# Selective scan of a fused four-layer block: TensorE makes the scan's input for both halves from dt*u turned beforehand

## The chip, the cores and the metric

The kernel runs on one core of a Trainium2 chip. The metric is the device time in microseconds (us) of the one launch that does everything. Engines are named as in the profile: PE is TensorE (its weight loads are PEld), DVE is VectorE, ACT is ScalarE, POOL is GpSimd, SP is SyncE, which issues DMAs. L1942 is line 1942 of the kernel before.

## The reference

The input is 4 sequences of 1024 tokens of 128 channels. Four layers follow one another, each on a layer norm of the running sum: attention, a mixture of 8 experts, a Mamba layer, a second mixture of experts. Only the Mamba layer matters here, cut to its core:

```python
xz = (x @ fc1_w.T + fc1_b) @ in_proj_w.T
xc, z = jnp.split(xz, 2, axis=-1)          # 256 inner channels each
u = silu(causal_conv4(xc, conv_w) + conv_b)
x_dbl = u @ x_proj_w.T                     # 8 columns for dt, 16 for B, 16 for C
dt = softplus(low8 @ dt_proj_w.T + dt_proj_b)
...                                        # for each of 16 states n, each channel c, along time t:
h[t] = exp(dt[t] * A[c, n]) * h[t - 1] + dt[t] * u[t] * B[t, n]
y[t] += h[t] * C[t, n]                     # summed over the 16 states
out = ((y + u * D) * silu(z)) @ out_proj_w.T @ fc2_w.T + fc2_b
```

## The kernel before, in words

Everything is float32 unless said otherwise. Each engine has its own instruction stream, written by hand, and semaphores order them; a block ends with a barrier of all engines. The Mamba layer is four blocks, one after another.

`mamba_in` (the input stage) works on 8 chunks of 512 tokens. The 256 inner channels are two halves of 128 partitions. Its first loop makes `u` and `silu(z)`. Its second loop makes, for each chunk: the low-rank product (`low_rank`, L1719: B, C and the 8 rows for dt, in one PSUM bank), `dt` (`project_dt`, L1726, then softplus as Abs, Exp and Ln on ACT at L1625 to L1630, `join` on DVE at L1674 and an addition on POOL at L1574), B turned so that tokens lie on partitions (`turn_b`, written inside `project_dt` at L1730, kept as `m.bt`), the rows of B and C written to DRAM (L1551), and B and C split into three bfloat16 parts whose sum is the float32 value (L1618, L1667, L1570, L1678, L1680; kept as `m.bc`).

`mamba_scan` (the scan stage) runs over 4 sequences x 16 states = 64 states, in pairs, and for each state over the two halves. A tile of one half and one state is 128 channels x 1024 tokens. For each of the 128 such tiles DVE runs one `tensor_tensor_scan` (L1942) along time. It needs two things: the decay, which ACT makes as exp(dt*A) (L1903), and the input dt*u*B. The two halves get their input in different ways:

- half 0: PE spreads the row of B over the partitions (`spread`, L1800: two bfloat16 matmuls of 96 rows and 512 columns), and DVE multiplies it in PSUM by dt*u (`scan_input`, L1932).
- half 1: PE makes the whole input (`make_x`, L1829): for each of 8 blocks of 128 tokens one float32 matmul with dt*u turned (tokens on partitions) as the stationary operand and a diagonal matrix of B as the moving one. ACT makes these diagonals (`diagonals`, L1883). The dt*u of the next sequence is made on POOL (L1982) and turned on PE one block at a time (L1812), stored by ACT (L1897).

After a scan POOL multiplies the state by the row of C (`weigh`, L1979), and PE adds the product into the running sum in PSUM (`add`, L1839, two float32 matmuls of 512 columns with the identity, for each tile). `skip` (L1846) adds u*D, twice in each sequence; `gate` on DVE (L1947) ends a sequence. The order of PE's stream in a pair is written out: add, spread, add, make_x, add, spread, add, make_x. The input banks in PSUM are single for each half: `spread` and `make_x` of the next state wait until the scan of this one has read them (`scanned`). `weigh` has one tile for each half, so it waits for `add` of the state before (`summed`).

The chunk order of the input stage's second loop is that of `ahead`: `low_rank` and `split` of chunk c+1 stand in front of `project_dt` and `join` of chunk c.

Of the kernel before, what the change touches and what calls it, by code (L numbers as in the profile page):

```python
# [15 lines left out]
P = 128  # L16
# [1453 lines left out]
def mamba_loads(nc, ctx, early, g):  # L1470
# [4 lines left out]
    m.sel_b = m.tensor("sel_b", [6 * NS, NS, P], g.w["sel_b"], BF16)  # L1475
# [3 lines left out]
    m.bc = sb("bc", [6 * NS, N], BF16)  # L1479
# [16 lines left out]
def mamba_in(nc, g, m):  # L1496

    with ExitStack() as ctx:
# [10 lines left out]
        rest = sb("rest", [2 * NS, 2, CH])  # L1509
        part1 = sb("part1", [2 * NS, 2, CH], BF16)  # L1510
# [7 lines left out]
        low_done, part0_ready, low_ready, rest_ready, part1_ready, part2_ready, dt_done, top_ready, soft_steps, dt_ready, a_steps = map(sem, (  # L1518
            "low_done", "part0_ready", "low_ready", "rest_ready", "part1_ready", "part2_ready", "dt_done", "top_ready",
            "soft_steps", "dt_ready", "a_steps"))  # L1520
        block = ctx.enter_context(nc.Block())
        CONV = KC * DI
        X_BANK, Z_BANK, LOW_BANK, DT_BANK, TURN_BANK = 0, 4, 0, 2, 6
# [19 lines left out]
        @block.sync  # L1543
        def _(sp):
            for k in range(2):
                sp.sem_inc(c_written[k], 16)
            with sp.Fori(0, B) as b:
                for k in range(CPB):
                    c = CPB * b + k
                    sp.wait_ge(whole_ready, c + 1)  # L1550
                    sp.dma_start(g.bc_rows[:, tokens(c)], bc_whole[:, k, :]).then_inc(c_written[k], 16)  # L1551
            for k in range(2):
                sp.wait_ge(c_written[k], 16 + 16 * B)

        @block.gpsimd
        def _(pool):
            pool.memset(xc[:, 0, :, 0:KC - 1], 0.0).then_inc(pad_set, 1)
            pool.wait_ge(m.loaded, m.all)

            pool.tensor_tensor(g.X[:, :, :], g.X[:, :, :], fc2_b[:, :].rearrange("p (a e) -> p a e", a=1).to_broadcast([P, NT, E]),  # L1560
                               ALU.add).then_inc(pool_seen, 1)

            with pool.Fori(0, B) as b:
                for k in range(CPB):
                    c = CPB * b + k

                    pool.wait_ge(part2_ready, c + 1)
                    pool.wait_ge(rest_ready, 2 + c + 1)
                    pool.sem_inc(pool_seen, 1)
                    pool.tensor_copy(part1[:, k, :], rest[:, k, :]).then_inc(part1_ready, 1)  # L1570
                    pool.wait_ge(top_ready, 2 + c + 1)
                    pool.wait_ge(soft_steps, 3 * (c + 1))
                    pool.sem_inc(pool_seen, 1)
                    pool.tensor_tensor(m.dt[:, :, tokens(c)], top[:, k, :, :], soft[:, k, :, :], ALU.add).then_inc(dt_ready, 1)  # L1574

        @block.scalar
        def _(act):
# [35 lines left out]
            def part0(b, k, c):  # L1613
                act.wait_ge(low_done, c + 1)
                act.wait_ge(c_written[k], 16 * b + 16)
                act.wait_ge(b_turned, c + 1)
                act.activation(bc_whole[:, k, :], PS[0:2 * NS, LOW_BANK + k, :], ACT.Copy).then_inc(whole_ready, 1)
                act.activation(m.bc[0:2 * NS, tokens(c)], PS[0:2 * NS, LOW_BANK + k, :], ACT.Copy).then_inc(part0_ready, 1)  # L1618

            def softplus(b, k, c):  # L1620

                act.wait_ge(dt_done, 2 + c + 1)
                act.wait_ge(dt_ready, c + 1)
# [7 lines left out]
            ahead(act, part0, softplus)  # L1631
            act.wait_ge(b_turned, 2 + NCH)
            act.activation(m.bt[:, :], PS[:, TURN_BANK, :], ACT.Copy).then_inc(a_steps, 1)
            act.wait_ge(a_steps, 3)

        @block.vector
        def _(dve):
            dve.sem_inc(conv_steps, 2 * CONV)
            dve.sem_inc(dt_ready, 2)
            dve.sem_inc(part2_ready, 2)  # L1640
# [19 lines left out]
            def split(b, k, c):  # L1660
                dve.wait_ge(low_done, c + 1)
                dve.wait_ge(dt_done, c - 1 + 2)
                dve.tensor_copy(low[2 * NS:, k, :], PS[2 * NS:2 * NS + R, LOW_BANK + k, :]).then_inc(low_ready, 1)
                dve.wait_ge(part0_ready, c + 1)
                dve.wait_ge(part1_ready, c + 1)
                dve.wait_ge(part2_ready, c + 1)
                dve.tensor_tensor(rest[:, k, :], PS[0:2 * NS, LOW_BANK + k, :], m.bc[0:2 * NS, tokens(c)], ALU.subtract).then_inc(rest_ready, 1)  # L1667

            def join(b, k, c):
                dve.wait_ge(dt_done, 2 + c + 1)  # L1670
                dve.wait_ge(dt_ready, c + 1)
# [5 lines left out]
                dve.wait_ge(rest_ready, 2 + c + 1)  # L1677
                dve.tensor_copy(m.bc[2 * NS:4 * NS, tokens(c)], rest[:, k, :])  # L1678
                dve.wait_ge(part1_ready, 2 + c + 1)
                dve.tensor_tensor(m.bc[4 * NS:6 * NS, tokens(c)], rest[:, k, :], part1[:, k, :], ALU.subtract).then_inc(part2_ready, 1)  # L1680
            ahead(dve, split, join)
            dve.wait_ge(a_steps, 2)
            dve.wait_ge(dt_ready, 2 + NCH)
            dve.wait_ge(part2_ready, 2 + NCH)

        @block.tensor
        def _(pe):
            pe.sem_inc(u_ready, 2 * DI)
            pe.sem_inc(dt_done, 2)
            pe.sem_inc(part1_ready, 2)  # L1690
            pe.sem_inc(z_ready, 2)
            pe.sem_inc(rest_ready, 2)
            pe.sem_inc(top_ready, 2)
            pe.sem_inc(b_turned, 2)
# [21 lines left out]
            def low_rank(b, k, c):  # L1716
                pe.wait_ge(rest_ready, c + 1)
                for half in range(DI):
                    last = pe.matmul(PS[0:2 * NS + R, LOW_BANK + k, :], x_proj[:, half, :], m.u[:, half, tokens(c)], start=half == 0, stop=half == DI - 1)  # L1719
                last.then_inc(low_done, 1)  # L1720

            def project_dt(b, k, c):
                pe.wait_ge(low_ready, c + 1)
                pe.wait_ge(top_ready, c + 1)
                for half in range(DI):
                    last = pe.matmul(PS[:, DT_BANK + 2 * k + half, :], dt_proj[2 * NS:, half, :], low[2 * NS:, k, :], start=True, stop=True)  # L1726
                last.then_inc(dt_done, 1)
                pe.wait_ge(whole_ready, c + 1)
                for i in range(TPC):
                    last = pe.matmul(PS[:, TURN_BANK, bass.ds(c * (TPC * NS) + i * NS, NS)], bc_whole[0:NS, k, i * P:(i + 1) * P], g.ident[0:NS, 0:NS],  # L1730
                                     start=True, stop=True)
                last.then_inc(b_turned, 1)
            ahead(pe, low_rank, project_dt)


def mamba_scan(nc, g, m):


    with ExitStack() as ctx:
# [3 lines left out]
        h = g.xnT[:, :].rearrange("p (k d t) -> p k d t", k=2, d=DI)  # L1743
        dtu, decay = sb("dtu", [P, DI, T]), sb("decay", [P, 2, DI, T])
        c_rows, ch = sb("c_rows", [P, C_RING, T]), sb("ch", [P, DI, T])
        diag = sb("diag", [P, DI, P])
        dtu_turns, b_diag = sb("dtu_turns", [P, 2, TB, P]), sb("b_diag", [P, 2, TB, P])
        b_spread, decay_ready, dtu_ready, other_dtu_ready, input_ready, scanned, ch_ready, summed, gated, diag_ready = map(sem, (
            "b_spread", "decay_ready", "dtu_ready", "other_dtu_ready", "input_ready", "scanned", "ch_ready", "summed", "gated", "diag_ready"))
# [602 lines left out]
```

## Time and profile before

| what | us |
|---|---|
| median of 3 runs (lowest, highest) | 1429.58 (1429.04, 1433.34) |
| the profiled execution, its own time | 1432.1 |
| its span, from the first to the last instruction | 1430.3 |
| second loop of the input stage: first low-rank matmul | at 813.10 |
| scan stage: first instruction | at 856.90 |
| scan stage: last gate begins | at 1256.57 |

The profiled execution lies 2.5 above the median, and its own time 1.8 above its span. Everything below is read on the axis of the span. PE is busy for 89% of the span, DVE for 78%, ACT for 58% and POOL for 41%. The mean clock granted to TensorE is 0.933 of full speed. A busy PE in the profile includes the modelled ends of matmuls, which overlap; the distance from start to start is what a group of matmuls takes.

### The profile page before, as it was taken

The page shows a single profiled execution, that of the slowest core. Times are in us where ns is not written, and L with a number is a line of the kernel's source. Part 1 is how long each engine was busy: PE and PEld are TensorE (multiplying, and loading weights), DVE is VectorE, ACT ScalarE, POOL GpSimd, SP SyncE. Part 2 cuts the span into 40 slices and gives each one's busy share as a digit, 9 for nine tenths or more (in the row PEclk, how much of TensorE's full clock was granted, in tenths as well). Part 3 has the DMA queues.
Part 4 walks back from the last instruction along what each step waited for, and adds up shares of the span by engine and source line. Part 5 has one row for each costly group of instructions (what it writes and reads, how often), then busy time and mean ns, then how long its engine had stood idle before and what let it go on. Part 6 is the DMA issues. An engine that isn't in the chain of part 4 may idle for free. (4 is left out here: it accounts for less than half of the span.)

```text
span 1430.3 us, 23953 instructions
## 1 busy us (share of the span) xinstructions
PE 1268.5 (89%) x8534; PEld 662.8 (46%) x8534; DVE 1111.4 (78%) x1328; ACT 830.7 (58%) x1596; POOL 590.2 (41%) x442
## 2 busy tenths in 40 slices
PE   4937899999899889899978779999999999966998
PEld 2412333333334445354444235655656655555565
DVE  4769899999898547756555888989999999954554
ACT  2524899899798632132224788777778778502221
POOL 2320000010102166556744067788798788720000
PEclk9966999999999989999997878999999999985999
DMA  4331111311211173234420003222222222110221
GB/s 108 113 109 35 54 54 52 109 60 50 76 44 42 41 175 105 88 108 117 115 60 15 4 13 102 89 89 87 87 78 89 89 89 89 59 29 11 67 60 42
DMA packets 70751, 103.76 MB, mean 73 GB/s; under 512 B 12734, under 2 KB 42246, under 8 KB 70646
## 3 DMA queue, kind: packets, MB, share of 16 engines
q1 hardware_dynamic: 69350, 101.05, 23.4%
q10 hardware_dynamic: 1296, 1.33, 0.4%
q8 instruction: 64, 1.05, 0.3%
q14 instruction: 41, 0.34, 0.1%
HBM read 88.32 MB, written 13.63 MB: 71 GB/s over the span
## 5 line engine op out<-in xcount | busy, mean ns | idle before, releaser
L638 DVE TENSOR_REDUCE att_found<-PS 128x2 f32<-128x1024 f32 (+2 forms) x288 | 333.2, 1219 | 18.9 <-PE PS L747 17.1
L714 ACT ACTIVATE att_prob<-PS 128x512 f32<-128x512 f32 x576 | 313.5, 596 | 46.2 <-PE PS L769 34.4
L1979 POOL TENSOR_TENSOR ms_ch<-xnT,ms_c_rows 128x1024 f32<-128x1024 f32 x128 | 300.3, 2366 | 81.9 <-PE PS L1839 68.5
L1942 DVE TENSOR_TENSOR_SCAN xnT<-ms_decay,PS 128x1024 f32<-128x1024 f32 x128 | 287.0, 2276 | 17.6 <-PE PS L1829 8.7
L1839 PE MATMUL PS<-ms_ch,ident_sb 128*128 128x512 f32 x512 | 241.5, 594 | 1.2 <-POOL ms_ch L1979 1.2
L788 PE MATMUL PS<-att_prob,att_v 128*32 128x256 f32 (+1 forms) x2560 | 184.9, 376 | 2.8 <-ACT fr_out L703 2.6
L1903 ACT ACTIVATE ms_decay<-m_dt,m_a 128x1024 f32<-128x1024 f32 x128 | 145.8, 1144 | 54.8 <-DVE xnT L1942 53.3
L1883 ACT ACTIVATE ms_b_diag<-ident_sb,m_bt 128x128 f32<-128x128 f32 x512 | 155.7, 387 | 0.0
L747 PE MATMUL PS<-kr,qr 55*128 55x128 bf16 (+4 forms) x1152 | 121.4, 292 | 30.9 <-PEq L260 15.7
L1829 PEld LDWEIGHTS PS<-ms_b_diag,ms_dtu_turns 128*128 128x128 f32 x1024 | 122.6, 194 | 32.0 <-issue 29.7
L1829 PE MATMUL PS<-ms_b_diag,ms_dtu_turns 128*128 128x128 f32 x1024 | 127.7, 279 | 6.6 <-issue 5.4
L769 PE MATMUL PS<-qr,kr 55*128 55x128 bf16 (+4 forms) x1152 | 115.5, 279 | 15.2 <-ACT att_prob L714 8.3
L1839 PEld LDWEIGHTS PS<-ms_ch,ident_sb 128*128 128x128 f32 x512 | 91.7, 190 | 75.1 <-issue 61.7
L1262 ACT ACTIVATE f_h<-PS,e_w_b 128x512 f32<-128x512 f32 x64 | 44.0, 687 | 138.2 <-PE PS L1413 135.0
L747 PEld LDWEIGHTS PS<-kr,qr 48*128 48x128 bf16 (+1 forms) x1152 | 39.7, 97 | 138.2 <-issue 88.8
L1243 POOL TENSOR_TENSOR f_yT<-f_yT,f_prod 128x512 f32<-128x512 f32 x56 | 71.0, 1268 | 70.8 <-DVE f_prod L1355 69.4
L1345 DVE SCALAR_TENSOR_TENSOR f_x3s<-PS,e_w_b,f_mask_row 128x512 f32<-128x512 f32 x64 | 48.0, 750 | 61.5 <-PE PS L1417 60.8
L1231 POOL TENSOR_TENSOR f_xm<-xnT,f_gate_row 128x512 f32<-128x512 f32 x64 | 81.2, 1270 | 13.3 <-DMA f_gate_row<-gate_rows_dram 9.8
L788 PEld LDWEIGHTS PS<-att_prob,att_v 128*32 128x32 f32 x2560 | 55.2, 109 | 63.1 <-issue 53.9
L1932 DVE TENSOR_TENSOR PS<-ms_dtu,PS 128x1024 f32<-128x1024 f32 x64 | 77.4, 1210 | 4.5 <-PE PS L1800 2.4
L1422 PE MATMUL PS<-f_h,e_w_w 128*128 128x512 f32 x128 | 66.3, 599 | 8.5 <-DVE f_prod L1355 8.4
L1413 PE MATMUL PS<-f_xm,e_w_w 128*128 128x512 f32 x128 | 67.8, 612 | 4.1 <-POOL f_xm L1231 4.1
(232 smaller groups left out, 1634.6 us busy)
## 6 DMA issues: line engine op xcount, KB each, us to landing
ms_c_rows<-bc_rows_dram SPq DMA_DIRECT2D x64, 512.0 KB, 3.6
f_gate_row<-gate_rows_dram SPq DMA_DIRECT2D x64, 256.0 KB, 3.4
f_mask_row<-mask_rows_dram SPq DMA_DIRECT2D x64, 128.0 KB, 3.1
qk_parts_dram<-qkv_parts SPq DMA_DIRECT2D x48, 128.0 KB, 1.9
heads_dram<-fr_out SPq DMA_DIRECT2D x16, 256.0 KB, 2.6
f_mask_row<-mask_rows_dram SPq DMA_DIRECT2D x64, 64.0 KB, 3.2
qr<-qk_parts_dram SPq DMA_DIRECT2D x32, 96.0 KB
qr<-qk_parts_dram SPq DMA_DIRECT2D x96, 32.0 KB
```

Source lines behind the costliest of these rows:

```text
L638: dve.tensor_reduce(found[:, :, pair, first:first + (n - 1) * step + 1:step], PS[:, bank:bank + 2, :].rearrange("p r (w n) -> p r w n", w= ...
L714: act.activation(prob[:, step % PROB_RING * GH + h, :], PS[:, SCORE_BANK + unit % SCORE_RING, :], ACT.Exp, scale=float(D) ** -0.5).then_in ...
L747: last = pe.matmul(PS[:, MAX_BANK + 2 * (m % 2) + r, at:at + n], rows(qr, count, i, pair, r, q_block * P, P), rows(kr, count, i, pair, r, ...
L769: last[r] = pe.matmul(PS[:, SCORE_BANK + (unit + r) % SCORE_RING, col:col + w], rows(kr, count, i, pair, r, j * P, P), rows(qr, count, i, ...
L788: last = pe.matmul(PS[VW * h:VW * (h + 1), VALUE_BANK, q - half * CH:q - half * CH + w], v1[:, i % 2, half, h, j, :], prob[:, step % PROB_ ...
L1231: pool.tensor_tensor(xm[:, e % XM_RING, :], xnT[:, c * CH:(c + 1) * CH], gate_row[:, e % ROW_RING, :], ALU.mult).then_inc(xm_ready, 1)
L1829: last = pe.matmul(PS[:, X_BANK + 2 + k // TPC, k % TPC * P:(k % TPC + 1) * P], dtu_turns[:, b % 2, k, :], b_diag[:, odd, k, :], start=Tru ...
L1839: last = pe.matmul(PS[:, Y_BANK + 2 * half + q, :], g.ident[:, :], ch[:, half, q * CH:(q + 1) * CH], start=j == 0 and not odd, stop=j == J ...
L1883: last = act.activation(b_diag[:, odd, i, :], g.ident[:, :], ACT.Identity, scale=m.bt[:, at:at + 1])
L1903: act.activation(decay[:, odd, half, :], m.dt[:, half, sequence(p // JB)], ACT.Exp, scale=m.a[:, half, n:n + 1]).then_inc(decay_ready, 1)
L1942: dve.tensor_tensor_scan(h[:, odd, half, :], decay[:, odd, half, :], inputs(half), 0.0, ALU.mult, ALU.add).then_inc(scanned, 1)
L1979: pool.tensor_tensor(ch[:, half, :], h[:, odd, half, :], c_rows[:, s % C_RING, :], ALU.mult).then_inc(ch_ready, 1)
```

## The change

In the input stage, the split of B and C into bfloat16 parts is gone, with its loads (`sel_b`, `m.bc`). Instead DVE multiplies dt by u (`times_u`, both halves of a chunk in one instruction), PE turns the product (`turn_dtu`, 8 transposes a chunk), and ACT stores the turned half 0 and DVE the turned half 1 (`store_turns`), for all four sequences. The low-rank product has one PSUM bank in place of two, and only the rows of C go to DRAM. In the scan stage PE makes the input of both halves by `make_x`; `spread`, `scan_input` and the turns inside the scan are gone. The scan writes the state over its decay, in a ring of three. A half is added 1.5 states (half 1: two) after the newest input in PE's stream. The ring of C rows has 4 places for 3. The diff, cut to its core:

```diff
 def mamba_in(nc, g, m):
...
+            def store_turns(c):
+                act.wait_ge(dtu_turned, DI * c + 1)
+                act.activation(m.dtu_turns[:, c * TPC:(c + 1) * TPC, 0, :], PS[:, DTU_BANKS[0], :].rearrange("p (i c) -> p i c", c=P),
+                               ACT.Copy).then_inc(dtu_stored[0], 1)
+
+            store_low(0)
+            for c in range(NCH):
+                if c + 1 < NCH:
+                    store_low(c + 1)
+                softplus(c)
+                if c >= 2:
+                    store_turns(c - 2)
...
+            def times_u(c):
+                dve.wait_ge(dt_ready, c + 1)
+                if c >= 2:
+                    dve.wait_ge(dtu_turned, DI * (c - 1))
+                dve.tensor_tensor(dtu[:, c % 2, :, :], m.dt[:, :, tokens(c)], m.u[:, :, tokens(c)], ALU.mult).then_inc(dtu_ready, 1)
...
+            split(0)
+            for c in range(NCH):
+                if c + 1 < NCH:
+                    split(c + 1)
+                join(c)
+                if c >= 1:
+                    times_u(c - 1)
+                if c >= 2:
+                    store_turns(c - 2)
...
+            def turn_dtu(c):
+                pe.wait_ge(dtu_ready, c + 1)
+                for half in range(DI):
+                    if c >= 1:
+                        pe.wait_ge(dtu_stored[half], c)
+                    for i in range(TPC):
+                        last = pe.transpose(PS[:, DTU_BANKS[half], i * P:(i + 1) * P], dtu[:, c % 2, half, i * P:(i + 1) * P], g.ident[:, :])
+                    last.then_inc(dtu_turned, 1)
...
 def mamba_scan(nc, g, m):
...
+            def make_x(s, half):
+
+                pe.wait_ge(b_diag_ready, through(s, 1))
+                if s > 0:
+                    pe.wait_ge(scanned, through(s - 1, half))
+                for k in range(TB):
+                    last = pe.matmul(PS[:, X_BANK + 2 * half + k // TPC, k % TPC * P:(k % TPC + 1) * P], m.dtu_turns[:, s // NS * TB + k, half, :],
+                                     b_diag[:, s % 2, k, :], start=True, stop=True)
+                last.then_inc(x_made, 1)
...
             pe.wait_ge(diag_ready, DI)
-            spread(0, 0)
-            first_turns()
             make_x(0, 0)
...
+            make_x(0, 1)
+            for s in range(STATES):
+                if s + 1 < STATES:
+                    make_x(s + 1, 0)
+                if s >= 2:
+                    add(s - 2, 1)
+                if s + 1 < STATES:
+                    make_x(s + 1, 1)
+                if s >= 1:
+                    add(s - 1, 0)
+            add(STATES - 2, 1)
+            add(STATES - 1, 0)
+            add(STATES - 1, 1)
...
+            for part in range(CPB):
+                diagonals(0, part)
+            for s in range(STATES):
+                for half in range(DI):
+                    decays(s, half)
+                    if s + 1 < STATES:
+                        diagonals(s + 1, half)
...
+            def scan(s, half):
+                dve.wait_ge(decay_ready, through(s, half))
+                dve.wait_ge(x_made, through(s, half))
+                dve.tensor_tensor_scan(decay_then_h(s, half), decay_then_h(s, half), inputs(half), 0.0, ALU.mult, ALU.add).then_inc(scanned, 1)
...
+            for s in range(STATES):
+                b, n = divmod(s, NS)
+                for half in range(DI):
+                    scan(s, half)
+                    if n == 1 and b > 0:
+                        gate(b - 1, half)
...
+            for s in range(STATES):
+                pool.wait_ge(c_in[s % C_RING], C_BASE + 16 * (s // C_RING + 1))
+                for half in range(DI):
+                    pool.wait_ge(scanned, through(s, half))
+                    if s >= 1:
+                        pool.wait_ge(summed, through(s - 1, half))
+                    pool.tensor_tensor(ch[:, half, :], decay_then_h(s, half), c_rows[:, s % C_RING, :], ALU.mult).then_inc(ch_ready, 1)
```

PE's stream in the middle of the scan stage before, over two states (a row is one instruction of the program with its line, what it writes and reads, and its shape; x8 means eight in a row):

```order
L1829 MATMUL PS<-ms_b_diag,ms_dtu_turns 128x128 x8
L1839 MATMUL PS<-ms_ch,ident_sb 128x512 x2
L1800 MATMUL PS<-m_bc,m_w_sel_b 128x512 x2
L1839 MATMUL PS<-ms_ch,ident_sb 128x512 x2
L1829 MATMUL PS<-ms_b_diag,ms_dtu_turns 128x128 x8
L1839 MATMUL PS<-ms_ch,ident_sb 128x512 x2
L1800 MATMUL PS<-m_bc,m_w_sel_b 128x512 x2
L1839 MATMUL PS<-ms_ch,ident_sb 128x512 x2
```

The same place after the change, over two states again (line 1825 is `make_x`, 1835 is `add`):

```order
L1825 MATMUL PS<-ms_b_diag,m_dtu_turns 128x128 x8
L1835 MATMUL PS<-ms_ch,ident_sb 128x512 x2
L1825 MATMUL PS<-ms_b_diag,m_dtu_turns 128x128 x8
L1835 MATMUL PS<-ms_ch,ident_sb 128x512 x2
L1825 MATMUL PS<-ms_b_diag,m_dtu_turns 128x128 x8
L1835 MATMUL PS<-ms_ch,ident_sb 128x512 x2
L1825 MATMUL PS<-ms_b_diag,m_dtu_turns 128x128 x8
L1835 MATMUL PS<-ms_ch,ident_sb 128x512 x2
```

In each state the two bfloat16 matmuls of `spread` have given their place to a second group of eight float32 matmuls of `make_x`; the two groups of `add` are still there.

DVE's stream at a like place before:

```order
L1932 TENSOR_TENSOR PS<-ms_dtu,PS 128x1024
L1942 SCALAR_TENSOR_TENSOR xnT<-ms_decay,PS 128x1024 x2
L1932 TENSOR_TENSOR PS<-ms_dtu,PS 128x1024
L1942 SCALAR_TENSOR_TENSOR xnT<-ms_decay,PS 128x1024 x2
L1932 TENSOR_TENSOR PS<-ms_dtu,PS 128x1024
```

And after (line 1889 is the scan, over three states of the ring, with line 1894, the gate, where a sequence ends):

```order
L1889 SCALAR_TENSOR_TENSOR xnT<-xnT,PS 128x1024 x4
L1889 SCALAR_TENSOR_TENSOR ms_one_state<-ms_one_state,PS 128x1024
L1894 TENSOR_TENSOR m_u<-PS,m_sz 128x1024
L1889 SCALAR_TENSOR_TENSOR ms_one_state<-ms_one_state,PS 128x1024
L1894 TENSOR_TENSOR m_u<-PS,m_sz 128x1024
```

The multiplication in front of every second scan is gone from DVE; two scans a state are left.

PE's stream in the input stage's second loop after the change, over two chunks (1732 is `low_rank`, 1742 `project_dt`, 1748 `turn_b`, 1758 `turn_dtu`):

```order
L1732 MATMUL PS<-m_u,m_w_x_proj 40x512 x2
L1742 MATMUL PS<-mi_low,m_dt_proj 128x512 x2
L1748 MATMUL PS<-ident_sb,mi_bc_whole 128x16 x4
L1758 MATMUL PS<-ident_sb,mi_dtu 128x128 x8
L1732 MATMUL PS<-m_u,m_w_x_proj 40x512 x2
L1742 MATMUL PS<-mi_low,m_dt_proj 128x512 x2
L1748 MATMUL PS<-ident_sb,mi_bc_whole 128x16 x4
L1758 MATMUL PS<-ident_sb,mi_dtu 128x128 x8
```

The first three rows of a chunk were there before (L1719, L1726, L1730); the eight transposes are new.

## Rows read from the trace of the kernel before

**Rows 1.** Groups by line, 861 to 1252 us: busy us, mean ns, idle before.

```profile
L1979 POOL TENSOR_TENSOR ms_ch<-xnT,ms_c_rows 128x1024 f32<-128x1024 f32 x127 | 298.0, 2366 | 81.9 <-PE PS L1839 68.5 <-DVE xnT L1942 13.1
L1942 DVE TENSOR_TENSOR_SCAN xnT<-ms_decay,PS 128x1024 f32<-128x1024 f32 x128 | 287.0, 2276 | 17.6 <-PE PS L1829 8.7 <-ACT ms_decay L1903 0.6
L1839 PE MATMUL PS<-ms_ch,ident_sb 128*128 128x512 f32 x504 | 237.5, 593 | 0.0
...
L1903 ACT ACTIVATE ms_decay<-m_dt,m_a 128x1024 f32<-128x1024 f32 x128 | 145.8, 1144 | 54.8 <-DVE xnT L1942 53.3
L1829 PE MATMUL PS<-ms_b_diag,ms_dtu_turns 128*128 128x128 f32 x1024 | 127.7, 279 | 6.6 <-issue 5.4 <-ACT ms_dtu_turns L1889 1.2
...
L1932 DVE TENSOR_TENSOR PS<-ms_dtu,PS 128x1024 f32<-128x1024 f32 x64 | 77.4, 1210 | 4.5 <-PE PS L1800 2.4 <-POOL ms_dtu L1982 2.0
...
L1846 PE MATMUL PS<-m_u,ms_diag 128*128 128x512 f32 x32 | 15.0, 592 | 0.0
```

**Rows 2.** Timeline of PE in the scan stage: start us, length us, line, count.

```profile
1020.52 1.95 PE L1829 MATMUL PS<-ms_b_diag,ms_dtu_turns 128*128 128x128 f32 x16
1022.31 1.88 PE L1839 MATMUL PS<-ms_ch,ident_sb 128*128 128x512 f32 x4
1024.03 0.60 PE L1800 MATMUL PS<-m_bc,m_w_sel_b 96*128 96x512 bf16 x2
1024.46 1.88 PE L1839 MATMUL PS<-ms_ch,ident_sb 128*128 128x512 f32 x4
1026.18 0.27 PE L1812 MATMUL PS<-ident_sb,ms_dtu 128*128 128x128 f32 x1
1026.29 1.95 PE L1829 MATMUL PS<-ms_b_diag,ms_dtu_turns 128*128 128x128 f32 x16
```

**Rows 3.** Windows: length, busy of PE, PEld, DVE, ACT, POOL, then granted clock.

```profile
751.00:757.00 6.00, 4.44 (x16) 2.86 (x16) 5.15 (x20) 1.93 (x4) 6.00 (x7) 0.50 0.36 82
...
827.00:832.00 5.00, 5.00 (x20) 1.75 (x19) 4.57 (x8) 4.91 (x8) 2.91 (x2) 1.00 0.05 13
...
842.00:847.00 5.00, 4.97 (x17) 2.74 (x18) 4.57 (x8) 4.71 (x8) 3.29 (x3) 0.50 0.10 26
...
900.00:1240.00 340.00, 333.63 (x1493) 199.25 (x1492) 320.12 (x174) 258.83 (x579) 271.53 (x117) 1.00 0.25 87
```

**Rows 4.** Timeline of the input stage's second loop, PE and DVE.

```profile
820.32 1.91 PE L1719 MATMUL PS<-m_u,m_w_x_proj 128*40 x4
...
824.07 1.91 PE L1719 MATMUL PS<-m_u,m_w_x_proj 128*40 x4
```

**Rows 5.** Timeline of the same loop, all engines.

```profile
834.53 1.41 DVE L1674 TENSOR_SCALAR mi_xc<-PS,m_w_dt_b 128x512 f32<-128x512 f32 x2 [0.29 <-ACT mi_conv L1625]
...
838.80 1.41 DVE L1674 TENSOR_SCALAR mi_xc<-PS,m_w_dt_b 128x512 f32<-128x512 f32 x2 [0.29 <-ACT mi_conv L1625]
...
850.20 1.26 ACT L1625 ACTIVATE mi_conv<-PS,m_w_dt_b 128x512 f32<-128x512 f32 x2 [0.37 <-PE PS L1726]
...
853.90 2.45 POOL L1574 TENSOR_TENSOR m_dt<-mi_xc,mi_conv 128x1024 f32 x1 [1.15 <-ACT mi_conv L1630]
```

**Rows 6.** Groups by line, 812 to 856.9 us.

```profile
L1628 ACT ACTIVATE mi_conv<-mi_conv 128x1024 f32<-128x1024 f32 x8 | 8.5, 1057 | 0.3
...
L1663 DVE COPY mi_low<-PS 8x512 f32<-8x512 f32 x8 | 5.5, 683 | 2.2 <-PE PS L1719 2.0
...
L1617 ACT ACTIVATE mi_bc_whole<-PS 32x512 f32<-32x512 f32 x8 | 4.6, 574 | 3.0 <-PE PS L1719 3.0
```

**Rows 7.** Timeline of the first microseconds of the scan stage.

```profile
856.95 2.81 DVE L1927 TENSOR_TENSOR ms_dtu<-m_dt,m_u 128x1024 f32<-128x1024 f32 x2 [2.79 <-PEq L1498]
858.21 2.45 ACT L1883 ACTIVATE ms_b_diag<-ident_sb,m_bt 128x128 f32<-128x128 f32 x8
...
862.70 3.78 PE L1829 MATMUL PS<-ms_b_diag,ms_dtu_turns 128*128 128x128 f32 x16 [1.23 <-ACT ms_dtu_turns L1889]
```

**Rows 8.** Timeline of the last gate of the scan stage.

```profile
1256.57 1.23 DVE L1947 TENSOR_TENSOR m_u<-PS,m_sz 128x1024 f32<-128x1024 f32 x1 [1.08 <-PE PS L1839]
```

More of the change, by code:

```diff
@@ L1561, in _ @@
                                ALU.add).then_inc(pool_seen, 1)
[L1563 to L1574, printed above, removed]
+            for c in range(NCH):
+                pool.wait_ge(top_ready, c + 1)
+                pool.wait_ge(soft_steps, 3 * (c + 1))
+                pool.tensor_tensor(m.dt[:, :, tokens(c)], top[:, c % 2, :, :], soft[:, c % 2, :, :], ALU.add).then_inc(dt_ready, 1)
         @block.scalar
@@ L1833, in add @@
-            def add(p, odd, half):
-                b, j = divmod(p, JB)
-                if j == 0 and not odd and b > 0:
-                    pe.wait_ge(gated, DI * (b - 1) + half + 1)
-                pe.wait_ge(ch_ready, scans(p, odd, half))
-                for q in range(CPB):
-                    last = pe.matmul(PS[:, Y_BANK + 2 * half + q, :], g.ident[:, :], ch[:, half, q * CH:(q + 1) * CH],
-                                     start=j == 0 and not odd, stop=j == JB - 1 and bool(odd))
+            def make_x(s, half):
[6 more added lines that the diff above has]
+                last.then_inc(x_made, 1)
@@ L1841, in add @@
+            def add(s, half):
+                b, n = divmod(s, NS)
+                if n == 0 and b > 0:
+                    pe.wait_ge(gated, through(b - 1, half))
+                pe.wait_ge(ch_ready, through(s, half))
+                for q in range(CPB):
+                    last = pe.matmul(PS[:, Y_BANK + 2 * half + q, :], g.ident[:, :], ch[:, half, q * CH:(q + 1) * CH], start=n == 0, stop=n == NS - 1)
                 last.then_inc(summed, 1)
[L1843 to L1846 removed]
+                if n == NS // 2 + half:
+                    for q in range(CPB):
+                        pe.matmul(PS[:, Y_BANK + 2 * half + q, :], diag[:, half, :], m.u[:, half, b * T + q * CH:b * T + (q + 1) * CH], start=False, stop=False)
@@ L1874, in _, with diagonals @@
             act.preload_act_table(ACT.Exp)
-            def diagonals(p, odd):
-                n, b = 2 * p % NS + odd, p // JB
-                if p > 0:
-                    act.wait_ge(x_made, states(p - 1, odd))
-                for i in range(TB):
+            def diagonals(s, part):
+                b, n = divmod(s, NS)
+                if s >= 2:
+                    act.wait_ge(x_made, through(s - 2, 1))
+                for i in range(part * TPC, (part + 1) * TPC):
                     at = NS * (TB * b + i) + n
-                    last = act.activation(b_diag[:, odd, i, :], g.ident[:, :], ACT.Identity, scale=m.bt[:, at:at + 1])
+                    last = act.activation(b_diag[:, s % 2, i, :], g.ident[:, :], ACT.Identity, scale=m.bt[:, at:at + 1])
```

310 lines of the change are left out of this document (87 added, 223 removed).

## The prediction, made before the changed kernel ran

> **What bounds the kernel now.** I read the page first. It ranks DVE's scan and PE's additions near the top and gives no stage. So I asked for the groups by line inside the scan stage, then for PE's timeline there, then for the windows with the granted clock, then for the timelines of the loop before it.
>
> The scan stage runs from 856.9 [rows 7] to the end of the last gate, 1256.57 + 1.23 = 1257.8 [rows 8]: 400.9 us. Over 64 states DVE spends 287.0 on scans and 77.4 on the multiplication for half 0 [rows 1], 5.76 a state (2 x 2.276 + 1.21). It looks like the bound: its idle time before scans is 17.6 in all. But PE is as full. From start to start in [rows 2], `make_x` takes 1022.31 - 1020.52 = 1.79, an `add` 1024.03 - 1022.31 = 1.72, `spread` 0.43, the other `add` 1.72, a transpose 0.11; then the next state's `make_x` starts. These five follow one another with no gap, and their sum is 5.77, from 1020.52 to 1026.29. So here PE and DVE are level at about 5.77 a state, and I read the busy share of PE (333.6 of 340 [rows 3]) as real and not as a product of modelled ends. POOL needs 2 x 2.37 = 4.73 a state and waits for `add` (68.5 in all), ACT 2 x 1.14 + 2.45 = 4.74 (two decays [rows 1], eight diagonals [rows 7]) and waits for the scans (53.3). Both have over one microsecond to spare.
>
> **The change, part by part.**
>
> *Scan stage, DVE.* 64 multiplications of 1.21 go: 77.4 less, 4.55 a state left. That is worth something only if nobody else needs 5.77.
>
> *Scan stage, PE.* A state loses `spread` (0.43) and, in 24 of the 64 states, a transpose of 0.11; it gains a second `make_x` of the same shape, operands and kind, 1.79. New cycle: 2 x 1.79 + 2 x 1.72 = 7.02, against 5.77. Times 64 that is 449.3. The `skip` matmuls stay: 32 records are 8 groups of 4, each as long as an `add`, so 13.8. PE's whole work is 463.1. Before it was 64 x 5.66 + 13.8 + 24 x 0.11 + about 2 for the first turns = 381, in a stage of 401; DVE's was 287.0 + 77.4 + 8 gates of 1.23 + 2.8 = 377. The 20 above these sums was lost because two full engines wait for one another through single input banks.
>
> Can PE run its 7.02 without gaps? Call t the end of `make_x`(s+1, half 0). Then PE has `add` (s-2, half 1) until t+1.72, `make_x`(s+1, half 1) until t+3.51, `add`(s-1, half 0) until t+5.23, and `make_x`(s+2, half 0), which wants scan(s+1, half 0): t to t+2.3, nearly 3 early. `make_x`(s+2, half 1) starts at t+8.7 and wants the other scan, over at t+5.8. `weigh`(s, half 0) can start at t+5.3 (its tile is free after the `add`), ends by t+7.7, and its `add` comes at t+10.5. The decays go into a tile whose `weigh` ended more than 9 before. So no wait is left in the steady state, DVE idles 2.5 a state, and what was lost to coupling should mostly not recur. Where a sequence ends, two gates stand between scans: DVE waits for the last `add` of half 0 (t+5.3), then for that of half 1 (t+8.8), so the next scans are late: about 0.3 of PE, three times, 1 in all.
>
> The in-place scan and the third ring place have no row. Bounds: nothing, and 1.22 more a scan (7.02 shared by two, less 2.28) before DVE would be the bound. I take nothing, since even half as much again would hide under PE.
>
> *Start and end.* The first `make_x` needs ACT's table load and eight diagonals: 1.28 + 2.45 [rows 7], so it starts about 3.9 after the stage's start. PE has been idle and its clock is low: the first `make_x` of before took 3.78 from 862.70 [rows 7] where it takes 1.79 later. I count the first two at that length, 4.0 more than in the sum. Filling costs 0.6 (the second state's `make_x` waits for the first scans), the end 3.5 (`weigh`, 2.37, is no longer covered between the last additions; from the last `make_x` the chain add, weigh, add, weigh, add is 13 to 14 long and the bare additions 10.3), and the last gate 1.4. Stage: 3.9 + 463.1 + 4.0 + 1 + 0.6 + 3.5 + 1.4 = 477.5, against 400.9: **+76.6**.
>
> *Input stage.* Before, PE alone could turn a chunk in 824.07 - 820.32 = 3.75 [rows 4], and the loop ran at 838.80 - 834.53 = 4.27 [rows 5], set by DVE and ACT. Now PE has 8 transposes more, 0.11 each: 4.63. ACT: 0.57 for the low rows, 1.26 + 1.06 + 1.06 of softplus [rows 5, 6], 0.57 for the turned half (the same 512 columns; half 0 of a chunk), with gaps 4.6. DVE: 0.68 + 1.41 + 1.40 (2.81 for two of 128x1024 [rows 7]) + 0.68 = 4.2. Three engines within 0.4 of one another, and one bank for the low rows where there were two: I take 4.8 a chunk, between 4.65 (PE without a wait) and 5.3. Over the 7 steps from the first to the last softplus, with the first `project_dt` a microsecond later than before because the second low-rank product waits for the bank, the last softplus begins at 854.7 for 850.20 [rows 5]. After it: 3.4 of softplus, 2.45 on POOL [rows 5] as before, and new behind it `times_u` 1.4, 8 transposes (1.9 at the low clock), a store 0.7. Before, the stage ended with POOL's addition. So 4.5 + 4.0 is 8.5, less 0.5 of gaps that overlap: **+8**, with bounds of 4 and 13.
>
> What goes from the input stage (two ACT and DVE copies, POOL's cast, the 384 KB load of `sel_b`) is counted in these cycles; the loads themselves ended under the normalisation and delayed nothing.
>
> **Sum.** 76.6 + 8 is 84.6. I shave 1 for the clock rising sooner in the first two `make_x` than I counted: +83.5. The profiled execution's own 1432.1 becomes 1515.6; on the median 1429.58 it is **1513**.
>
> A rule weighed against this. The loop of the normalisation does only transposes on PE, and its granted clock is 0.50 [rows 3], the lower of the two levels (1.2 GHz), though PE is busy 4.44 of 6.00 there. In the input stage before, the clock was full from 817 and fell to 0.50 once PE had begun to wait for DVE in each chunk [rows 3]. The Trainium skill, "TensorE: Matmul & The Clock Gate", Part 4 (PE-mode transpose), says that transposes do not count as PE-busy for the clock in the way that matmuls do. The row of the normalisation agrees. By that rule the eight transposes a chunk would be a pause to the clock in every chunk; it makes the second rival below likelier.
>
> **The rivals.**
>
> *The clock falls in the input stage* (0.2). Before, it fell after four chunks with the PE at 3.75 of 4.27. If the new loop loses it too, a chunk costs PE 2 x 4.63 = 9.3 for 4.8, and four chunks cost 18 more: 1531. For it: the low window at 842 and the transposes. Against: PE is now nearly the slowest engine of this loop and hardly waits. With two such chunks it is 1522.
>
> *The scan stage couples after all* (0.1). The addition of half 1 now comes late, and `weigh` waits for it. If POOL were late by 0.2 a state (rows: it runs 4.73 of 7.02, so this needs handovers of more than a microsecond each), the stage is 13 longer: 1526.
>
> *Faster: PE was not full* (0.03). If the starts in [rows 2] only show PE pushed by DVE's pace and the second `make_x` fitted into slack, DVE's 4.55 would rule: 64 x 1.21 = 77 less, 8 more of input stage, 1360. It decides at the point where two `make_x` and two additions together take less than 5.77; for that `make_x` would have to cost 1.17. Against: a stretch of float32 matmuls with no gap between groups, at full clock, has no slack to give.
>
> *No net change* (0.02): `make_x` at 1.17 to 1.2, or DVE losing more to coupling before than I see. The same evidence speaks against it.
>
> The rest, 0.65, is the forecast, 1513, whose own bounds are 1504 (input stage +4, no loss at the boundaries and at the end) and 1521 (input stage +13, 0.05 more a state).
>
> **How the numbers follow.** Likeliest 1513. The range reaches from 1503 to 1530: it takes in the forecast's bounds, the coupling rival and the clock falling for up to four chunks, and leaves out the two rivals of 0.03 and 0.02 and the far tail of the slow ones. 0.3% (4.3 us) is about what a measurement of this kernel can tell from no change. Slower 0.95, same 0.02, faster 0.03.
>
> **What would show it.** After the change: PE's timeline in the scan stage with a start of `make_x` every 3.51 and of a state every 7.02, no idle time before them; DVE idle about 2.5 a state and waiting for `make_x`; POOL and ACT waiting longer than before; the stage near 477. In the input stage a `join` about every 4.8, and three new steps after POOL's last addition. Wrong would be: starts of `make_x` closer than 1.79 before the next group; PE idle in the middle of the stage, released by POOL or by DVE; a clock under 1.00 between 900 and 1300; scans longer than 2.28.

## The result: 1512.0 us, 5.7% slower

The changed kernel takes 1511.99 us (median of 4 runs, 1510.47 to 1516.04), the kernel before 1429.9 in the same comparison. The ratio is 1.0574, with a 95% interval of 1.0546 to 1.0602. Forecast were 1513 and slower.

The profiled execution has a span of 1509.0 for 1430.3, 78.7 more. It can be cut at three points that both traces have: the table load of ACT that opens the input stage's second loop, the one that opens the scan stage, and the end of the last gate.

| stretch | before, us | after, us | difference |
|---|---|---|---|
| up to the second loop's table load | 813.1 | 810.1 | -3.0 |
| second loop of the input stage | 43.8 | 49.9 | +6.1 |
| scan stage | 400.9 | 475.9 | +75.0 |
| behind the last gate | 172.5 | 173.1 | +0.6 |

The -3.0 is no effect of the change: 2.4 of it are there where the transposes ahead of the input stage begin (at 751.83 before, 749.46 after), and in the profiled executions of all the runs below that first table load lies anywhere from 807.2 to 815.2, with nearly the same code ahead of it. The cut points after, from the timeline:

```profile
810.07 1.28 ACT L1597 ACT_TABLE_LOAD   x1
...
859.96 1.28 ACT L1859 ACT_TABLE_LOAD   x1 [1.52 <-PEq L1497]
...
1334.64 1.23 DVE L1894 TENSOR_TENSOR m_u<-PS,m_sz 128x1024 f32<-128x1024 f32 x1 [1.08 <-PE PS L1835]
```

PE's timeline after, in the middle of the scan stage, answers to [rows 2]:

```profile
1100.01 1.88 PE L1835 MATMUL PS<-ms_ch,ident_sb 128*128 128x512 f32 x4
1101.72 1.95 PE L1825 MATMUL PS<-ms_b_diag,m_dtu_turns 128*128 128x128 f32 x16
1103.51 1.88 PE L1835 MATMUL PS<-ms_ch,ident_sb 128*128 128x512 f32 x4
1105.23 1.95 PE L1825 MATMUL PS<-ms_b_diag,m_dtu_turns 128*128 128x128 f32 x16
1107.01 1.88 PE L1835 MATMUL PS<-ms_ch,ident_sb 128*128 128x512 f32 x4
```

From 1100.01 to 1107.01 is one state, 7.00, of four groups of 1.71 to 1.79, with no gap. The windows (PE, PEld, DVE, ACT, POOL, granted clock) and the groups by line say who waits:

```profile
880.00:1310.00 430.00, 429.71 (x2405) 307.51 (x2404) 277.94 (x125) 275.35 (x595) 279.11 (x119) 1.00 0.22 72
```

```profile
L1835 PE MATMUL PS<-ms_ch,ident_sb 128*128 128x512 f32 x512 | 241.1, 594 | 1.8 <-POOL ms_ch L1917 1.8
L1917 POOL TENSOR_TENSOR ms_ch<-xnT,ms_c_rows 128x1024 f32<-128x1024 f32 x86 | 202.9, 2360 | 117.5 <-PE PS L1835 108.0 <-DVE xnT L1889 9.4
L1889 DVE TENSOR_TENSOR_SCAN xnT<-xnT,PS 128x1024 f32<-128x1024 f32 x86 | 196.3, 2285 | 107.5 <-PE PS L1825 107.2
L1867 ACT ACTIVATE ms_b_diag<-ident_sb,m_bt 128x128 f32<-128x128 f32 x500 | 158.8, 388 | 110.0 <-PE PS L1825 110.0
```

PE is busy for 429.7 of 430 at full clock; DVE, ACT and POOL have each over 100 us of idle time that ends with a matmul. DVE gave up 77 us of multiplications and got them back as waiting.

### The profile page after: what moved, and what is told of

Its sections match the earlier page's. It is cut to its first block and busy times, and to the rows that moved or that the text cites. A ratio compares the mean times of both kernels' runs of the same rounds, so it can differ in the third digit from the quotient of the medians.

```text
span 1509.0 us, 25474 instructions
## 1 busy us (share of the span) xinstructions
PE 1356.4 (90%) x9462; PEld 770.6 (51%) x9462; DVE 1041.9 (69%) x1254; ACT 830.0 (55%) x1570; POOL 574.1 (38%) x428
## 5 line engine op out<-in xcount | busy, mean ns | idle before, releaser
L1825 PEld LDWEIGHTS PS<-ms_b_diag,m_dtu_turns 128*128 128x128 f32 x2048 | 250.2, 193 | 67.1 <-issue 65.4
L1889 DVE TENSOR_TENSOR_SCAN xnT<-xnT,PS 128x1024 f32<-128x1024 f32 x86 | 196.3, 2285 | 107.5 <-PE PS L1825 107.2
L1825 PE MATMUL PS<-ms_b_diag,m_dtu_turns 128*128 128x128 f32 x2048 | 252.2, 277 | 6.5 <-ACT ms_b_diag L1867 5.2
L1917 POOL TENSOR_TENSOR ms_ch<-xnT,ms_c_rows 128x1024 f32<-128x1024 f32 x86 | 202.9, 2360 | 117.5 <-PE PS L1835 108.0
L1867 ACT ACTIVATE ms_b_diag<-ident_sb,m_bt 128x128 f32<-128x128 f32 x512 | 162.5, 388 | 110.1 <-PE PS L1825 110.0
L1889 DVE TENSOR_TENSOR_SCAN ms_one_state<-ms_one_state,PS 128x1024 f32<-128x1024 f32 x42 | 95.9, 2285 | 49.1 <-PE PS L1825 49.0
L1835 PEld LDWEIGHTS PS<-ms_ch,ident_sb 128*128 128x128 f32 x512 | 87.6, 191 | 66.8 <-issue 61.7
L1917 POOL TENSOR_TENSOR ms_ch<-ms_one_state,ms_c_rows 128x1024 f32<-128x1024 f32 x42 | 99.0, 2357 | 52.5 <-PE PS L1835 52.5
L1874 ACT ACTIVATE xnT<-m_dt,m_a 128x1024 f32<-128x1024 f32 x86 | 98.1, 1141 | 33.5 <-POOL ms_ch L1917 33.5
```

Source lines behind the costliest of these rows:

```text
L1825: last = pe.matmul(PS[:, X_BANK + 2 * half + k // TPC, k % TPC * P:(k % TPC + 1) * P], m.dtu_turns[:, s // NS * TB + k, half, :], b_diag[: ...
L1835: last = pe.matmul(PS[:, Y_BANK + 2 * half + q, :], g.ident[:, :], ch[:, half, q * CH:(q + 1) * CH], start=n == 0, stop=n == NS - 1)
L1867: last = act.activation(b_diag[:, s % 2, i, :], g.ident[:, :], ACT.Identity, scale=m.bt[:, at:at + 1])
L1874: act.activation(decay_then_h(s, half), m.dt[:, half, sequence(b)], ACT.Exp, scale=m.a[:, half, n:n + 1]).then_inc(decay_ready, 1)
L1889: dve.tensor_tensor_scan(decay_then_h(s, half), decay_then_h(s, half), inputs(half), 0.0, ALU.mult, ALU.add).then_inc(scanned, 1)
L1917: pool.tensor_tensor(ch[:, half, :], decay_then_h(s, half), c_rows[:, s % C_RING, :], ALU.mult).then_inc(ch_ready, 1)
```

## The experiments

Each ratio compares a run with the kernel before on the same chip. Experiments 1 and 4 to 6 ran on one chip, 2, 7, 9 and 10 on a second, 3 and 8 on a third, and of each there is one profile. Stage means the scan stage, from the table load to the end of the last gate, in the profiled execution; it is set against the 400.9 before and the 475.9 after.

**1. A multiplication more on DVE, in every state** (changed kernel, ring of C rows at 3):

```diff
...
+                dve.tensor_tensor(spare[:, :], m.dt[:, 0, sequence(b)], m.sz[:, 0, sequence(b)], ALU.mult).then_inc(spare_set, 1)
                 for half in range(DI):
                     scan(s, half)
```

> The changed kernel, with one more DVE multiplication of 128x1024 in front of the scans of every state (64 in all, into a tile that nobody reads) and the ring of C rows at 3 places for want of space. Theory (PE alone sets the pace of the scan stage, 7.02 us a state, and DVE idles some 2.4 of them): no more than 2 us slower than the changed kernel, since DVE goes from 4.57 to about 5.8 a state. Rival (the engines couple through the single input banks, so DVE's time still counts): 20 to 80 us slower, with starts of make_x further apart than 3.51.

Measured: ratio 1.0669 (1.0616 to 1.0722), stage 487.4, 11.5 more than the changed kernel's. Neither theory said that: the instruction was not the one that I had counted. Its group:

```profile
L1901 DVE TENSOR_TENSOR ms_spare<-m_dt,m_sz 128x1024 f32<-128x1024 f32 x63 | 165.6, 2629 | 0.0
```

At 2.63 for 1.2 to 1.4, DVE came to 7.2 us a state (2 x 2.28 + 2.63), over PE's 7.0, so this run says nothing on DVE's slack. The second loop of the input stage, whose code is that of the changed kernel, also took 56.6 us for 49.9, since the clock fell early in it (windows; the clock stands third from the end):

```profile
817.00:822.00 5.00, 4.74 (x19) 1.80 (x19) 2.09 (x3) 4.58 (x7) 1.06 (x1) 1.00 0.01 2
822.00:827.00 5.00, 5.00 (x15) 2.26 (x13) 3.23 (x4) 3.00 (x4) 3.21 (x2) 0.53 0.06 13
827.00:832.00 5.00, 5.00 (x12) 2.16 (x12) 2.78 (x4) 3.87 (x5) 0.86 (x2) 0.50 0.00 0
832.00:837.00 5.00, 5.00 (x25) 2.40 (x24) 1.76 (x4) 2.67 (x4) 1.62 (x1) 0.95 0.04 10
```

**2. Half the size** (`spare[:, 0:CH]` from 512 columns):

> As the run with a DVE multiplication more in every state, but of 128x512 in place of 128x1024. In that run the extra instruction took 2.63 us in the mean and not the 1.2 to 1.4 that I had counted, which took DVE to 7.2 us a state, over PE's 7.02. At half the size it should take about 1.3 and DVE comes to 5.9. Theory (PE alone sets the pace): the scan stage is within 2 us of the 475.9 of the changed kernel. Rival (any DVE work costs through the single banks): 10 us or more above it.

Measured: ratio 1.0625 (1.0596 to 1.0654), stage 482.0, so 6.0 more. The instruction took 2.30 in the mean. The timelines of DVE and POOL show what it waits for:

```profile
1064.45 2.77 DVE L1901 TENSOR_TENSOR ms_spare<-m_dt,m_sz 128x512 f32<-128x512 f32 x1
```

```profile
1064.32 2.36 POOL L1921 TENSOR_TENSOR ms_ch<-xnT,ms_c_rows 128x1024 f32<-128x1024 f32 x1 [1.45 <-PE PS L1836]
```

It ends at 1067.22, 0.54 after POOL's at 1066.68. Still no clean test, with DVE at 6.9 a state.

**3. The extra multiplication with one operand in PSUM** (1.22 each, as `scan_input` was):

```diff
                 dve.wait_ge(x_made, through(s, half))
+                if half == 0:
...
+                    dve.tensor_tensor(spare[:, :], inputs(0), m.sz[:, 0, sequence(s // NS)], ALU.mult).then_inc(spare_set, 1)
```

> The changed kernel with one more DVE multiplication of 128x1024 in every state, which reads one operand from PSUM (the input of half 0, before its scan) and one from SBUF, as the multiplication of the kernel before did, and writes a tile that nobody reads; ring of C rows at 3. The two earlier runs took both operands from SBUF: their extra instructions lasted 2.6 us at 128x1024 and 2.3 us at 128x512, since they did not end before POOL's multiplication beside them, and DVE came to 6.9 to 7.2 us a state. This one should take 1.22. Theory (PE alone sets the pace): DVE comes to 5.8 a state and the scan stage stays within 2 us of 475.9. Rival (DVE's time counts through the single banks): 10 us or more above.

Measured: ratio 1.0593 (1.0564 to 1.0623), whose interval overlaps the changed kernel's; stage 481.2, so 5.3 more: over the 2 of the theory and under the 10 of the rival. In the steady state a half state keeps its pitch (`make_x` starts at 1068.01 and the next one at 1071.52: 3.51, half of 7.0). PE's waits for the scans are 5.9 in all, for 1.0 in the changed kernel: 0.9 at each of the three places where a sequence ends and another begins, where the changed kernel has no wait over 0.2, and 3.0 for 0.9 in the first states. So 78 us of DVE work cost 5: in the middle of a sequence DVE's time is hidden, and at the start and at those ends it is not. No run has the ring of C rows at 3 places and nothing else; the pitch of 3.51 shows that it costs nothing in the steady state.

**4. Half of one `make_x`** (changed kernel; half 0 scans a half stale input):

```diff
-                for k in range(TB):
+                for k in range(TPC if half == 0 else TB):
```

> The changed kernel, with make_x of half 0 making only 4 of its 8 blocks; the rest of the input bank is left as it is, so half 0 of the scan reads stale input. Theory (PE's work is the stage): a state costs 7.02 less 4 x 0.223 = 6.13, so 64 x 0.89 = 57 us less, 1455 us. Rival (coupling or POOL and ACT near the bound): less than 40 us less.

Measured: ratio 1.0223 (1.0193 to 1.0253), some 1461 for 1512; stage 422.9, 53.1 less. A state costs 6.11. What is taken from PE comes out of the time. Some 4 us of the 57 are missing. PE's waits for scans have that size: 1.0 at each of the three ends of a sequence, where the changed kernel has none over 0.2, and 2.9 for 0.9 in the first states.

**5. The kernel before without DVE's multiplication** (half 0 scans B alone):

```diff
...
-                dve.tensor_tensor(inputs(0), dtu[:, 0, :], inputs(0), ALU.mult).then_inc(input_ready, 1)
...
```

> The kernel before, without the 64 DVE multiplications of half 0: its scan reads B as it was spread, without dt*u. Theory (PE was as full as DVE, so taking work from DVE alone buys only what the two lost to one another): PE keeps 5.66 a state and 381 us of work in a stage of 401; 8 to 18 us faster than before. Rival (DVE was the bound, and PE only seemed busy): 64 x 1.21 = 77 us faster.

Measured: ratio 0.9967 (0.9948 to 0.9987), stage 399.5, 1.4 less. Far from 77, and my 8 to 18 missed too. PE's states stay at 5.77, and DVE waits for `make_x`:

```profile
1003.20 1.95 PE L1829 MATMUL PS<-ms_b_diag,ms_dtu_turns 128*128 128x128 f32 x16
...
1008.96 1.95 PE L1829 MATMUL PS<-ms_b_diag,ms_dtu_turns 128*128 128x128 f32 x16
```

```profile
DVE xnT L1939 <- PE PS L1829: 70.1, 53, 2.9
```

The last line is from the view of waits: us in total, times, longest. The 1.4 is partly the clock's. In this run it was granted in full later in the stage (0.50 from 864 to 868, 13 to 17 us after the table load, where before it stood at 1.00 from 869 to 873, 12 to 16 us after it): the second `make_x` and the `add` behind it took 3.54 and 2.93 from start to start, for 1.86 and 1.72 before, 2.9 more. Without that the stage would be some 4 shorter, an estimate; it is still no 8.

**6. The kernel before with ring, later sums and later gates** (`spread` and the multiplication stay):

```diff
...
+            for s in range(STATES):
...
+                of(spread, s + 1)
...
+                add_then_skip(s - 2, 1)
...
+                of(make_x, s + 1)
...
+                add_then_skip(s - 1, 0)
...
```

> The kernel before with only the other parts of the scan's change: the state written over its decay in a ring of three, the sums one state later in PE's stream, the gates one state later; half 0 keeps spread and DVE's multiplication, and the input stage stays as before. Theory (PE and DVE are both at 5.77 a state, and the stage loses some 20 us where sequences end, at the skips, at its start and its end): 3 to 12 us faster than before. Rival (the looser order does nothing, or its longer tail costs): no change or up to 3 us slower.

Measured: ratio 1.0411 (1.0382 to 1.044), stage 461.7, 60.8 more. Neither theory had that. The waits name two places: DVE waited 6.5 three times for dt*u of the next sequence, which POOL makes behind a `weigh` that now comes later, and the second half of `make_x` waited for a stored turn, at 6.8 us a state:

```profile
904.55 1.88 PE L1845 MATMUL PS<-ms_ch,ident_sb 128*128 128x512 f32 x4
...
910.35 1.16 PE L1835 MATMUL PS<-ms_b_diag,ms_dtu_turns 128*128 128x128 f32 x8 [0.77 <-ACT ms_dtu_turns L1905]
911.35 1.88 PE L1845 MATMUL PS<-ms_ch,ident_sb 128*128 128x512 f32 x4
```

**7. The same without dt*u and turns for the later sequences** (they scan the first one's input again):

```diff
...
-                turns = b + 1 < B and 0 <= i < TB
+                turns = False
...
```

> The run in which the kernel before got only the in-place ring, the later sums and the later gates, 59 us slower than before; here without dt*u and its turns for the second to fourth sequence (they scan the first one's input again). Theory on that loss (the transposes inside make_x and POOL's dt*u stand behind work that the later sums delay: ACT stores a turn behind a decay that waits for weigh, a state of 6.80 us for 5.77 in 24 states, and three waits of 6.5 us for dt*u of the next sequence): the loss goes, stage within 8 us of the 400.9 of before. Rival (the order itself, with PE at 5.66 and sums a state behind, costs): a stage of 420 or more.

Measured: ratio 1.017 (1.0149 to 1.0192), stage 427.2. 34.5 of the 60.8 are gone, 26.3 stay. The theory wanted the stage within 8 of 400.9 and the rival 420 or more, so by its own bounds the theory failed: the two waits are over half of the loss and not all of it. PE's waits for `ms_b_diag` (14.4 in 27 times) pointed at the rest: I had left ACT's stream as it was, with the diagonals of a state behind decays that now wait for a `weigh` (1.17 in each of the states looked at).

**8. The whole order**, ACT's stream too, and dt*u of half 0 in two tiles:

```diff
...
+            for s in range(STATES):
+                if s > 0:
+                    decays(s // 2, s % 2, 0)
+                    store_turn(s // 2, s % 2)
+                decays(s // 2, s % 2, 1)
+                if s + 1 < STATES:
+                    diagonals((s + 1) // 2, (s + 1) % 2)
...
```

> The kernel before with the whole order of the change in the scan stage, and with what stood in its way moved: ring of three in place, sums one state later, gates one state later, as before; and now ACT's stream in the order of the change (decays of a state, then the diagonals of the next), a turn stored between the two decays of its state, and dt*u of half 0 in two tiles, made early in a sequence. Half 0 keeps spread and DVE's multiplication. Theory (in the two runs with the new order the diagonals stood in ACT's stream behind decays that wait for weigh of the state before the last; with ACT in step the order itself costs nothing, and it frees what is lost where sequences end): a stage of 390 to 400 for 400.9, so 1 to 11 us faster than before. Rival (the order costs by itself with PE at 5.66 us a state): a stage of 415 or more.

Measured: ratio 1.0012 (0.9998 to 1.0026), stage 406.8, between the theory's 390 to 400 and the rival's 415. Of the 60.8, 5.9 are left, the states are at 5.77 again, and a sequence takes 97.8 from gate to gate, for 97.95 before: no gain. The 5.9 lie at the two ends of the stage. From the last `make_x` to the end it takes 16.4 for 11.8, since four sums are left there in place of two that wait for `weigh` (the last pair of gates waits 8.5 and 1.1, for 3.7 and 1.1 before). At the start the first three states take 2.0 more; the clock stood at 0.50 for longer there. The run moved ACT's stream, the stored turns and dt*u at once, so it doesn't show the share of each.

**9 and 10. Cheap sums.** The product of state and C row is stored as float16 and added with a float16 identity; PSUM stays float32. Each product is thereby rounded.

```diff
-        c_rows, ch = sb("c_rows", [P, C_RING, T]), sb("ch", [P, DI, T])
+        c_rows, ch = sb("c_rows", [P, C_RING, T]), sb("ch", [P, DI, T], mybir.dt.float16)
...
-                    last = pe.matmul(PS[:, Y_BANK + 2 * half + q, :], g.ident[:, :], ch[:, half, q * CH:(q + 1) * CH], start=n == 0, stop=n == NS - 1)
+                    last = pe.matmul(PS[:, Y_BANK + 2 * half + q, :], ident16[:, :], ch[:, half, q * CH:(q + 1) * CH], start=n == 0, stop=n == NS - 1)
```

On the changed kernel:

> The changed kernel, with the product of state and C row stored as float16 and added with a float16 identity, so that an addition takes 0.43 us of PE for 1.72 (the sum in PSUM stays float32; each product is rounded to 11 bits). Theory (DVE's freed time is real and only hidden under PE): PE falls from 7.02 to 4.44 us a state, and POOL (2 x 2.36 = 4.73), ACT (4.73) and DVE (4.57) are next, all at once: a stage of 320 to 345 for 475.9, so 1355 to 1385. Rival (the stage couples, or POOL slows with the other type): over 360, so over 1395.

Measured: 1370.96, ratio 0.9597 (0.9568 to 0.9625), stage 330.3. It beats both kernels. PE's timeline in states without `skip`, and DVE's beside it:

```profile
903.92 1.95 PE L1826 MATMUL PS<-ms_b_diag,m_dtu_turns 128*128 128x128 f32 x16
905.70 0.59 PE L1836 MATMUL PS<-ms_ch,ms_ident 128*128 128x512 f16 x2
906.19 2.02 PE L1826 MATMUL PS<-ms_b_diag,m_dtu_turns 128*128 128x128 f32 x16
...
908.48 1.95 PE L1826 MATMUL PS<-ms_b_diag,m_dtu_turns 128*128 128x128 f32 x16
```

```profile
899.19 9.06 DVE L1890 TENSOR_TENSOR_SCAN xnT<-xnT,PS 128x1024 f32<-128x1024 f32 x4
```

A state takes 4.56 (903.92 to 908.48), which is two scans one right behind the other: DVE sets the pace there. PE alone would need 4.44. POOL's two products take 4.66 a state where they follow one another with no gap (from 906.92 to 916.23 for four); it falls behind and catches up at the `skip`s and where a sequence ends.

On the kernel before:

> The kernel before with the same float16 products and identity. Theory: PE falls from 5.66 to 3.1 us a state, and DVE, at 5.76 a state and 377 in all, becomes the bound: a stage of 385 to 392 for 400.9, 9 to 16 us faster than before. So with cheap sums the change would be a gain of 30 us or more, the other sign than with float32 sums. Rival (PE was not what held DVE): no change.

Measured: 1421.27, ratio 0.9931 (0.9908 to 0.9954), stage 391.4. With float32 sums the change costs 82 us; with float16 sums on both sides it gains 50 (1421.3 to 1371.0). The change is the same; PE's cost around it decides the sign. The granted clock was 0.91 between 880 and 1240 in experiment 10 and 1.00 between 880 and 1180 in experiment 9, but the sign doesn't hang on it: experiment 10's states stay at 5.72 in most of the stage, and DVE's work there adds up to 377, so the clock can have cost at most 14 of the 61 by which the two stages differ.

## Why the prediction was right

**What bounds the kernel.** Right in the main point: PE was full before, and its busy share was real. Experiment 5 shows it: without any of DVE's multiplications for half 0 the states stay at 5.77 and the stage is 1.4 shorter. Wrong in a side one: I put the 20 us between PE's work (381) and the stage (401) down to two full engines that wait for one another. In the middle of a sequence they lose nothing, 5.77 being the sum of PE's groups. PE's timeline before shows where the 20 are:

```profile
868.98 2.02 PE L1829 MATMUL PS<-ms_b_diag,ms_dtu_turns 128*128 128x128 f32 x16 [1.64 <-issue]
...
1154.24 1.95 PE L1829 MATMUL PS<-ms_b_diag,ms_dtu_turns 128*128 128x128 f32 x16
...
1161.68 2.02 PE L1829 MATMUL PS<-ms_b_diag,ms_dtu_turns 128*128 128x128 f32 x16 [1.24 <-issue]
...
1168.53 2.02 PE L1829 MATMUL PS<-ms_b_diag,ms_dtu_turns 128*128 128x128 f32 x16
```

The second `make_x` starts 12.1 after the stage's start, with 3.5 of work in front of it at full clock: 8.5 go to the first fill and the low clock. Where a sequence ends, two states take 7.44 and 6.85 for 5.66: 3.0, three times, and here DVE, with two gates to run, does hold PE (the `spread` behind 1161.68 waits 0.88 for a scan). From the last `make_x` (1246.01) to the end there are 11.8 for 8.7 of work: 3. With DVE's multiplications gone (experiment 5) an end of a sequence costs 1.9, and in the changed kernel 0.34 (starts of `make_x` 3.76 and 3.58 apart for 3.50), which is the 1 in all that the prediction has for it.

**PE's sum.** 7.02 a state predicted, 7.00 measured. Experiment 4 takes 57 of PE's work away and the stage falls by 53; experiment 9 takes 165 and it falls by 146, down to DVE's two scans (4.56 a state). Stage +76.6 predicted, +75.0 measured. Of the 1.6 between them, 1.3 is the 0.02 a state, and 1.3 more lies in the first two groups of `make_x`: I counted 4.0 more for the low clock, and both together took 6.30 from 863.84, some 2.7 more than 2 x 1.79, as the clock rose sooner. The sum shaves 1 for just that; the other terms together were 1 too small.

**DVE and the in-place scan.** 2.285 a scan for 2.276. Taken at nothing, and right; DVE's slack is real in the steady state and small at the start and where gates stand (experiment 3, +5). The description of the change puts a half's sum 1.5 states (half 1: two) behind the newest input. In the program's order both halves' sums stand 2.5 states behind their own input (1.5 before); the prediction's working of the waits goes by the right order.

**The input stage.** +8 predicted, +6.1 measured. The pitch in the middle was 4.77, for the 4.8 taken, as PE's timeline shows:

```profile
831.99 1.91 PE L1732 MATMUL PS<-m_u,m_w_x_proj 128*40 128x512 f32 x4
...
835.74 1.09 PE L1758 MATMUL PS<-ident_sb,mi_dtu 128*128 128x128 f32 x8
836.77 1.91 PE L1732 MATMUL PS<-m_u,m_w_x_proj 128*40 128x512 f32 x4
```

What I had wrong is that all seven steps take that long. From softplus to softplus they took 3.82, 4.00, 4.82, 4.77, 4.77, 4.78 and 3.82: the first chunks have no transposes, and the last has no low-rank product. So the last softplus came 2.0 later against the loop's start, for the 4.5 predicted. The tail of three new steps was 4.0, as counted.

**The rivals.** The falling clock did not come in the profiled execution of the changed kernel, nor in those of experiments 3, 4 and 9; it came in those of 1 and 2, over some 10 us, and cost 6.7 each time (56.6 for 49.9), with the same instructions. So, as far as these six executions show, it is a matter of the execution; that it stayed away from the one that was profiled is luck that the 0.2 allowed for. The price that I gave for two chunks was 9. The Trainium skill ("TensorE: Matmul & The Clock Gate", Part 4) would make the transposes its cause. The traces here speak against it as the start of the fall: in experiment 1 the clock stands at 0.53 between 822 and 827, and the first transpose of the loop starts at 827.7. What else starts it stays open. (The prediction says that this rule makes the second rival likelier; it is the first that it means.) Coupling after all is ruled out in the changed kernel (PE is idle for 8.3 us in the whole stage, 3.9 of them before its first matmul). That PE was not full is ruled out by experiments 4 and 5.

**Luck.** The two stages together came to +81.1, for the +84.6 of the sum. The profiled execution ended 4.8 under its forecast of 1515.6, 2.4 of that in the code around the two stages (-3.0 and +0.6). The medians differ by 82.1, and 1513 against 1512.0 looks closer than the terms are.

## What to carry to other kernels

Where two engines are both near full, taking work from one and giving more than its slack to the other moves the time by what is added to the second one; so read the distance from start to start of the groups on the receiving engine before moving work there. Eight float32 matmuls on PE (1.79) are no cheap replacement for 1.21 on DVE and 0.43 of bfloat16 matmuls. When a move fails for this reason, look for the cheapest other work on the full engine: here the sums, at 220 of the 463 us of PE's work, and with those cheapened the same move pays.

## What the runs showed of the hardware that I had not expected

A DVE multiplication with both operands in SBUF is held up by POOL's multiplication. At 128x512 it took 0.66 at the least and 2.49 in the median, and at 128x1024 1.19 and 2.71, while the same size with one operand in PSUM took 1.22 beside the same POOL work. In 58 of the 64 cases of each run POOL had begun first, and DVE's instruction ended 0.55 (128x512) or 1.08 (128x1024) after POOL's, whenever it had begun itself. Once in each run DVE began 0.16 ahead, and then it was POOL's that took longer, 2.73 and 3.26 for 2.36. The Trainium skill ("SBUF — State Buffer", SBUF: two separate sides) says that such an instruction and one of GpSimd take a shared pair of ports in turn, each for its whole length; both traces agree with it. I had not applied it to my own experiment.

Later sums made the scan stage 61 us longer in a kernel whose other streams still assumed the old order, and 5.9 longer once those were moved along.

How soon the clock rises at the start of the scan stage differs from run to run: by the windows about 11 us after the table load before, 18 in experiment 5 and 21 in experiment 8, whose first instructions there are the same. That alone moved the stage by 2.9 in experiment 5. So a difference of 1 to 3 us between two stages, each read from one profile, shows little.
